# The first eight value gathers of the edge sums issued a stage earlier, and one one-hot matrix read out of another

## The reference, cut to what matters

```python
origin, destination = (edge_index[0], edge_index[1])
ws = scores * edge_weights                        # (E, 8 heads)
e = jnp.exp(ws - seg_max[origin])
denom = jax.ops.segment_sum(e, origin, num_segments=N)
att = e / (denom[origin] + 1e-16)
weighted_values = att[:, :, None] * v[destination]  # (E, 8, 64)
values = jax.ops.segment_sum(weighted_values, origin, num_segments=N)
```

## Time and profile before

| | |
|---|---|
| time, median of 3 runs | 1857.03 us (1853.54 to 1858.75) |
| span of the profiled execution | 1849.3 us |
| mean granted TensorE clock | 0.921 |
| busy: PE, DVE, POOL | 1576.9, 1142.3, 782.0 us |
| `edge_softmax` | from 587 to 626 us |
| `edge_sums` | from 626 to 907 us |

### The profile page before, as it was taken

The page is one execution under the profiler, slowest core; times in us unless marked ns, Lnnn a source line. Parts: engine busy times, 40 slices in busy tenths (PEclk is TensorE's granted clock), DMA queues, the critical chain, the costliest instruction groups (busy, mean ns, idle before and its releaser), DMA issues. The chain is left out here.

```text
span 1849.3 us, 22498 instructions
## 1 busy us (share of the span) xinstructions
PE 1576.9 (85%) x6671; PEld 968.2 (52%) x6671; DVE 1142.3 (62%) x2675; ACT 529.1 (29%) x1083; POOL 782.0 (42%) x723
## 2 busy tenths in 40 slices
PE   5797999577776699999696897998999999989976
PEld 5443546343433244444375664456787845845565
DVE  8788342688888599999757223447345251076545
ACT  4400314322223211221222332213223235345542
POOL 1677877566662367777342222205314200043200
PEclk8799999789886899999798998999999999989998
DMA  6123202766663256666513543320020100000002
GB/s 145 38 62 95 34 5 62 228 188 193 183 193 114 80 165 198 193 196 185 189 62 120 165 131 100 113 85 1 12 80 24 33 1 1 23 1 1 1 1 84
DMA packets 102744, 174.95 MB, mean 95 GB/s; under 512 B 38835, under 2 KB 49741, under 8 KB 102505
## 3 DMA queue, kind: packets, MB, share of 16 engines
q0 software_dynamic: 35440, 100.52, 20.0%
q1 hardware_dynamic: 67193, 72.97, 11.9%
HBM read 141.91 MB, written 31.36 MB: 94 GB/s over the span
## 5 line engine op out<-in xcount | busy, mean ns | idle before, releaser
L1260 POOL DMA_INDIRECT s_vbuf<-v_dram,s_recs x166 | 194.1, 1169 | 107.4 <-DVE s_vw L1288 57.0
L934 POOL DMA_INDIRECT s_kbuf<-k_dram,s_recs x166 | 158.4, 954 | 96.0 <-DVE s_prod L995 49.7
L1304 PE MATMUL s_acc<-s_vw,s_ohf 128*128 128x512 f32 x332 | 186.5, 644 | 1.0 <-DVE s_vw L1288 1.0
L1031 PE MATMUL s_psQ<-s_qh,s_ohT 128*128 x166 | 97.7, 588 | 62.7 <-issue 43.0
L995 DVE TENSOR_TENSOR s_prod<-s_psQ,s_kbuf 128x512 f32<-128x512 f32 x166 | 113.4, 683 | 45.6 <-remote 25.1
L1300 PE MATMUL s_acc<-s_ohd,s_ohb 128*128 128x512 bf16 (+1 forms) x498 | 118.7, 348 | 17.2 <-DVE s_ohf L1286 14.5
L675 POOL DMA_INDIRECT rec_dram<-s_rec,s_rowid x84 | 113.3, 1349 | 34.5 <-issue 29.5
L385 POOL DMA_INDIRECT rec_dram<-s_rec,s_rowid x76 | 91.7, 1207 | 76.4 <-issue 76.4
L1300 PEld LDWEIGHTS s_acc<-s_ohd,s_ohb 128*128 128x128 bf16 x498 | 48.3, 97 | 138.0 <-issue 118.3
L1288 DVE TENSOR_TENSOR s_vw<-s_vbuf,s_W 128x512 f32<-128x512 f32 x166 | 113.8, 686 | 1.1 <-DMA s_vbuf<-v_dram,s_recs 1.1
L969 DVE TENSOR_REDUCE s_W<-s_prod 128x8 f32<-128x512 f32 x166 | 112.2, 676 | 0.0
(11 more groups left out here) (524 smaller groups left out, 3529.4 us busy)
## 6 DMA issues: line engine op xcount, KB each, us to landing
s_wall<-in_L_ffn_W SPq DMA_DIRECT2D x16, 512.0 KB
y_slots<-s_y SPq DMA_DIRECT2D x27, 256.0 KB
AT_dram<-s_A SPq DMA_DIRECT2D x10, 640.0 KB
s_w<-in_L_mix_WqkvT SPq DMA_DIRECT2D x3, 1024.0 KB
s_kbuf<-k_dram,s_recs POOLq DMA_INDIRECT x166
s_vbuf<-v_dram,s_recs POOLq DMA_INDIRECT x166
rec_dram<-s_rec,s_rowid POOLq DMA_INDIRECT x160
k_dram<-s_xn_rows SPq DMA_DIRECT2D x10, 256.0 KB
```

What stands on the lines that cost most here:

```text
L934: nc.gpsimd.indirect_dma_start(out=kbuf[t % KB][:, :], out_offset=None, in_=b.k_dram, in_offset=bass.IndirectOffsetOnAxis(ap=recs[:, t, 2: ...
L1031: nc.tensor.matmul(psQ[t % 4][:, :], lhs, qh[:, bass.ds(g, 1), :].rearrange("p t d -> p (t d)"), start=True, stop=False)
L1260: nc.gpsimd.indirect_dma_start(out=vbuf[t % VB][:, :], out_offset=None, in_=b.v_dram, in_offset=bass.IndirectOffsetOnAxis(ap=recs[:, t, 2: ...
L1304: nc.tensor.matmul(into(3, D), ohf[i][:, :], vw[i][:, :], start=False, stop=False, skip_group_check=True).then_inc(s.used, 1)
```

## The change

1. The ring `vbuf` and its arrival semaphores are made before `edge_softmax` and live until the end of `edge_sums` in a scope of their own, `b.ring`, which is closed there: one more `clear` and barrier. To make room, the buffers `M` of `edge_softmax` lie over `AT`, which is not in use yet.
2. POOL issues the gathers of tiles 0 to 7 in `edge_softmax`, behind its one copy. In `edge_sums` it starts with tile 8.
3. `ohb` isn't made any more. A float32 1.0 has the bit pattern 0x3F800000, whose upper half is the bfloat16 1.0; so PE reads every second half word of `ohf` as the bfloat16 one-hot. Four of the five weight loads of a tile then have a step of two elements.

```diff
+    VB = 8
+    b.ring = top.enter_context(ExitStack())
+    psb, _, _ = b.tools(b.ring, "")
+    b.vbuf = [psb(f"vbuf{i}", [P, D]) for i in range(VB)]
+    b.v_arrived = [b.semaphore(f"v_in{i}") for i in range(VB)]
...
-        M = [sb(f"M{q}", [P, G, P]) for q in range(2)]
+        M = [b.over("AT", f"M{q}", [P, G, P], F32, q * G * P) for q in range(2)]
...
             nc.gpsimd.tensor_copy(b1[:, :, :], b.cols[:, 8:8 + KC].unsqueeze(2).broadcast_to([P, KC, P])).then_inc(s.row1, 1)
+            for t in range(VB):
+                gather_values(b, t)
...
+def gather_values(b, t):
+
+    k = t % len(b.vbuf)
+    b.nc.gpsimd.indirect_dma_start(out=b.vbuf[k][:, :], out_offset=None, in_=b.v_dram,
+                                   in_offset=bass.IndirectOffsetOnAxis(ap=b.recs[:, t, 2:3].bitcast(I32), axis=0)
+                                   ).then_inc(b.v_arrived[k], 16)
...
-        ohb = [sb(f"ohb{i}", [P, P], BF16) for i in range(2)]
+        ohb = [ohf[i][:, :].bitcast(BF16)[:, 1::2] for i in range(2)]
...
-            for t in range(TILES):
-                if t >= VB:
-                    pool.wait_ge(made[t % 2], (t - VB) // 2 + 1)
-                nc.gpsimd.indirect_dma_start(out=vbuf[t % VB][:, :], out_offset=None, in_=b.v_dram,
+            for t in range(VB, TILES):
+                pool.wait_ge(made[t % 2], (t - VB) // 2 + 1)
+                gather_values(b, t)
...
-                nc.vector.tensor_scalar(ohb[i][:, :], b.iota_h[:, 0:P], recs[:, t, 0:1], None, ALU.is_equal)
...
-                    nc.tensor.matmul(into(k, cw), ohb[i][:, :], ohd[i][:, c0:c0 + cw], start=False, stop=False, skip_group_check=True)
+                    nc.tensor.matmul(into(k, cw), ohb[i], ohd[i][:, c0:c0 + cw], start=False, stop=False, skip_group_check=True)
...
+    b.ring.close()
     b.mid.close()
```

More of the change, by code:

```diff
@@ L1229, in edge_sums @@
         sb, ps, s = b.tools(ctx, "zeroed made0 made1 oh0 oh1 used ready kept counts rounded stored split cv")
-        VB = 8
-        arrived = [b.semaphore(f"v_in{i}") for i in range(VB)]
+        vbuf, arrived, VB = b.vbuf, b.v_arrived, len(b.vbuf)
         made, oh_s = (s.made0, s.made1), (s.oh0, s.oh1)
         ohf = [sb(f"ohf{i}", [P, P]) for i in range(2)]
-        ohb = [sb(f"ohb{i}", [P, P], BF16) for i in range(2)]
+        ohb = [ohf[i][:, :].bitcast(BF16)[:, 1::2] for i in range(2)]
         ohd = [sb(f"ohd{i}", [P, NP], BF16) for i in range(2)]
         vw = [sb(f"vw{i}", [P, D]) for i in range(2)]
-        vbuf = [sb(f"vbuf{i}", [P, D]) for i in range(VB)]
         W3 = sb("W3", [P, ST, 3 * H], BF16)
@@ L1256, in _ @@
         def _(pool):
-            for t in range(TILES):
-                if t >= VB:
-                    pool.wait_ge(made[t % 2], (t - VB) // 2 + 1)
-                nc.gpsimd.indirect_dma_start(out=vbuf[t % VB][:, :], out_offset=None, in_=b.v_dram,
-                                             in_offset=bass.IndirectOffsetOnAxis(ap=recs[:, t, 2:3].bitcast(I32), axis=0)
-                                             ).then_inc(arrived[t % VB], 16)
+            for t in range(VB, TILES):
+                pool.wait_ge(made[t % 2], (t - VB) // 2 + 1)
+                gather_values(b, t)
         @block.vector
@@ L1299, in _ @@
                 for k, (c0, cw) in enumerate(CH):
-                    nc.tensor.matmul(into(k, cw), ohb[i][:, :], ohd[i][:, c0:c0 + cw], start=False, stop=False, skip_group_check=True)
+                    nc.tensor.matmul(into(k, cw), ohb[i], ohd[i][:, c0:c0 + cw], start=False, stop=False, skip_group_check=True)
                 den = acc[:, bass.ds(g & 1, 1), 2, 256:256 + 3 * H].rearrange("p s w -> p (s w)") if t else acc[:, 0, 2, 256:256 + 3 * H]
-                nc.tensor.matmul(den, ohb[i][:, :], W3[:, t, :], start=False, stop=False, skip_group_check=True)
+                nc.tensor.matmul(den, ohb[i], W3[:, t, :], start=False, stop=False, skip_group_check=True)
                 pe.wait_ge(made[i], u + 1)
```

## The result

The changed kernel takes 1848.22 us in the median of four runs (1845.52 to 1849.15), the kernel before 1856.57 us beside it. The ratio is 0.9953, with a 95% interval from 0.9941 to 0.9965: 8.35 us less, where the forecast had 10.1 less. The profiled execution spans 1843.6 us against 1849.3.

A forecast was written before the change was run, and what follows sets the result against it. PE was taken to bound the steady tiles of edge_sums, with DVE close behind. The terms -2.4 - 1.1 - 7.1 + 0.5 give -10.1 us, from 1857.0 to 1846.9 us, with a range from 1843 to 1857.

The forecast's parts named there:

- PE stays the bound, steady tiles 0: Steady tiles of edge_sums: PE keeps 1.51 us a tile, DVE without ohb only waits longer; 0 us.
- Splits, -2.4: At seven splits in edge_sums, PE's wait for ohf falls by 0.34 us each; -2.4 us.
- First tile, -1.1: Start of edge_sums: without ohb and the wait for the first gather, PE's float32 passes start earlier; -1.1 us.
- The stumble, -7.1: Tiles 6 to 9 of edge_sums: the delay behind POOL's dense first gathers goes entirely; -7.1 us.
- Gathers in `edge_softmax`, 0: Eight gathers moved into edge_softmax run on an otherwise idle POOL and empty DMA queues; 0 us.
- rival D: POOL's gathers hold DVE up in edge_softmax, at worst 7.6 us, leaving 1854.5 us, no change; chance 0.09.
- Clearing and barrier, +0.5: One more clearing and barrier costs between 0 and 0.96 us; +0.5 us taken.
- Strided loads, 0: PE's bfloat16 weight loads at a step of two half words stay covered by matmuls; 0 us, upper end +13.3.
- rival C: Strided weight loads over the covered 0.11 us lengthen every tile; at 190 ns +13.3 us, 1860.2 us; chance 0.12.

The follow-up runs named there:

- onehot_only: The kernel before with ohb read out of ohf instead of made by DVE, all gathers still issued in edge_sums; ratio 0.9991.
- look4: The kernel before with POOL's gathers only four tiles ahead of vw instead of eight; ratio 0.997.
- prefill_only: The changed kernel with DVE still making ohb, so against the kernel before only the ring is filled earlier, in edge_softmax; ratio 0.9962.
- before_paced: The kernel before with POOL's gather for tile t waiting until PE has ended tile t-8, instead of for DVE; ratio 0.998 to the kernel before.
- paced: The changed kernel with POOL's gather for tile t waiting until PE has ended tile t-8, instead of for DVE; 1843.66 us, ratio 0.9937.
- step2: The changed kernel with the elements of ohf 8 bytes apart, so the bfloat16 view is as sparse; 1845.5 us in one run.
- three_buffers: The changed kernel with three buffers each of ohf, ohd and vw instead of two; ratio 0.9973 to the kernel before.
- three_paced: The changed kernel with three buffers each of ohf, ohd and vw, and POOL's gathers waiting for PE instead of DVE; 1837.24 us, ratio 0.9902.

## Why the prediction was right, and where it was not

- **PE stays the bound, steady tiles 0:** right. A tile takes 1.511 us in both kernels.
- **Splits, -2.4:** -2.1 (8.7 to 6.6), and -2.4 in onehot_only, which does this alone.
- **First tile, -1.1:** mis-sized a little. From the memset to the start of tile 0's second float32 pass it is 5.66 us before and 3.93 after, -1.7, and another 1.0 is saved at tiles 1 and 2. In the second profile of the changed kernel the first is 4.65: -1.0.
- **The stumble, -7.1:** right in size (tiles 6 to 9 held 7.1 us, and nothing after), and that POOL's first series causes it is now shown. The stumble stays with that series (onehot_only) and goes when the series is cut short or moved (look4, prefill_only, the changed kernel). That its density is the reason is only in part so: in before_paced, where most of the series came at 1.3 to 1.5 us, 5.1 of 9.5 us stayed. The prediction's words that gathers would never be closer than 1.5 us were too strong: 18 of 157 distances are under 1.4 us.
- **Gathers in `edge_softmax`, 0:** mis-sized. It is +0.5 in one profile, +2.6 in the other, with +2.6 in prefill_only and +2.8 in paced. It does not look like rival D: DVE's operations beside gather 7 start at once and take 0.35 and 0.32 us, against 0.33 and 0.32 before; only the copy that waits for PE's result is late. The eight gathers also took until 606 us and not until 598. The Trainium skill, "SBUF — State Buffer", tells of the same pair in its box on DMAs issued by GpSimd: while DVE runs an operation in a mode with two ports, GpSimd can't write the descriptors, and the DMA seems blocked. The trace agrees in the gathers of 3.59 us beside DVE's scans of 3.09; no run shows which ports the scans take, and the first gather, which lies wholly beside a float32 copy of 2.64 us, kept its 0.97 us.
- **Clearing and barrier, +0.5:** +0.4, by the distance of the clearings at the end of `edge_sums`.
- **Strided loads, 0:** right, and rival C's condition is measured too: loads of 113 ns leave the tile at 1.517 us, and those of 144 ns (with float32 ones of 319) make it 1.63.
- **What the sum lacked:** late steps, +4.8 us. The prediction took the steady part of the earlier trace rows, POOL tied to DVE, as safe. It is not: wherever POOL follows DVE at tiles of 1.51 us, 2.1 (step2) to 5.6 us are lost in it in all profiles but that of before (0.4), and 13.1 with three buffers, where DVE can run further ahead. Tied to PE it is 0.0 to 0.8. The operation taken off DVE is not needed for it: look4, with `ohb` still made and nothing moved, has 5.6 us. Why the kernel before has so little stays open.

The terms as measured, -2.1 - 1.7 - 1.0 - 7.1 + 0.4 + 4.8 + 0.5, give -6.2 us; the two profiled spans differ by 5.7, the medians by 8.35. So the forecast's 10.1 was too much by the late steps and `edge_softmax`, and partly made up by the start: that 1848.2 came so near to 1846.9 is in part luck. The 7.7 us between span and median were also read wrongly, as what lies around the span. In every run that gives both, a time is only 1.8 to 2.5 us above its span, so the profiled execution of the kernel before was, by my estimate, some 5 us faster than its median; that of the changed kernel (1845.52) was 2.7 us faster than its own. This is where the spans' 5.7 and the medians' 8.35 part.

What stays open is the path between POOL and PE. That POOL's gathers delay what PE signals to DVE is shown by what removes it; no row shows what they contend for, and distance alone does not say when. Slow register instructions of PE are no full account: four of 385 to 702 ns stand in the stumble of the kernel before, but none over 150 ns in before_paced, look4 or the kernel after, where DVE starts late as well. The load of the DMA engines alone does not explain it: in the kernel before it is 0.69 to 0.72 from 632 to 646 us, around the stumble, and 0.84 from 720 to 724 us, where no step is late.

## What to carry to other kernels

When one engine issues indirect DMAs ahead for a pipeline, look at which signal paces it. Here it paid most to tie the gathers to the engine that is the bound, not to the one that uses the data: from the changed kernel a single wait was worth some 3 us (not clear of noise), and together with a third buffer 9, while the third buffer without it was worth nothing. And an edit that frees an engine off the bound is worth its cost only at the places where the bound waits for it; count those. Where such an engine gets room to run ahead, as DVE did with the third buffer, ask what it sets loose.

## What the runs showed of the hardware

- Beside series of indirect gathers on POOL at 1.25 us, some of PE's register instructions take some 700 ns instead of 46, one 1392: 33 over 150 ns in three_buffers, with series of up to seven, and 20 in three_paced, with series of three to five.
- DVE sits idle for passes of PE that are drawn as long ended: 2.77 us in the stumble before, 3.67 in onehot_only; with gathers 1.5 us apart, 2.28 in the kernel after.
- With a gather issued beside it, DVE's copy in `edge_softmax` starts 1.1 to 1.95 us behind the end of the matmuls that it waits for; without, 0.04 us.
- A gather beside DVE's scans takes up to 3.59 us instead of 0.95, and the scans keep their 3.09.
- A weight load of 128 columns in bfloat16 takes 97, 98, 113 and 144 ns in the mean at steps of 2, 4, 8 and 16 bytes; in float32 it takes 192, 197 and 319 at 4, 8 and 16.
